# A new order of the steps in a three-batch software pipeline: a decoder of two layers on one Trainium2 core

## The reference

```python
x = ln(x + L0_attn(x))          # Nystrom attention, 16 heads of 8, 64 landmarks,
                                # 6 steps of an iterative inverse
x = ln(x + L0_xattn(x, ctx))    # cross attention, 16 heads of 8, relative bias
x = ln(x + L0_ffn(x))           # 8 experts, top 1, relu
x = ln(x + L1_attn(x))          # causal attention, 16 heads of 8
x = ln(x + L1_xattn(x, ctx))    # cross attention, 16 heads of 64, mask, its own norm
x = ln(x + L1_ffn(x))           # gelu MLP, weights composed of 32 low-rank pieces
# iterative inverse, n_iter = 6
KV = K @ V
V = (0.25 * V) @ (13 * I - KV @ (15 * I - KV @ (7 * I - KV)))
```

## Time and profile before

| | |
|---|---|
| median of 3 runs | 2584.53 us (2582.13 to 2587.29) |
| the profiled execution, its time | 2582.42 us |
| the profiled execution, its span | 2580.6 us |
| mean granted TensorE clock | 0.951 |
| PE busy | 2279.9 us |
| DVE busy | 1957.8 us |
| ACT busy | 1443.2 us |
| POOL busy | 360.0 us |

### The profile page before, as it was taken

How to read it: one execution, slowest core, us unless ns; L and a number is a source line. 1 busy time by engine, 2 the same in 40 slices (tenths; PEclk the granted TensorE clock), 3 DMA queues, 4 the chain that set the end, 5 groups by cost and what they waited for, 6 DMA issues and landing times.

```text
span 2580.6 us, 95561 instructions
## 1 busy us (share of the span) xinstructions
PE 2279.9 (88%) x40576; PEld 1845.7 (72%) x40576; DVE 1957.8 (76%) x6185; ACT 1443.2 (56%) x5093; POOL 360.0 (14%) x516
## 2 busy tenths in 40 slices
PE   6589999999999999999999999999999999999875
PEld 4467777777777777777777777777777777777763
DVE  3358887887888887788888777888877788887753
ACT  0346565655665556566555655655565565656531
POOL 0001111111111111111111111111111111111111
PEclk9589999999999999999999999999999999999995
DMA  6000000000000000000000000000000000000000
GB/s 267 5 4 7 9 9 8 9 9 5 7 9 9 9 9 9 5 7 8 8 9 8 9 5 8 8 8 9 8 9 5 8 8 9 9 8 7 4 5 3
DMA packets 29529, 35.73 MB, mean 14 GB/s; under 512 B 3240, under 2 KB 27824, under 8 KB 28464
## 3 DMA queue, kind: packets, MB, share of 16 engines
q1 hardware_dynamic: 29104, 29.62, 3.3%
HBM read 27.51 MB, written 2.10 MB: 11 GB/s over the span
## 4 chain that ended last, share of the span: by engine, by line
PE 44%; DVE 29%; ACT 18%; issue 6%; POOL 1%; DVEq 0%; ACTq 0%; POOLq 0%
PE ps L525 23%; PE ps L528 7%; ACT probs L1079 5%; PE ps L785 3%; ACT ss L993 3%; PE ps L869 3%; PE ps L802 3%; DVE probsT L1322 2%; ACT probs L1027 2%; PE ps L917 2%; ACT ey L1004 2%; DVE small L1227 2%; DVE x_rows L1186 2%; DVE small L1315 2%; DVE qk_v L1310 1%
## 5 line engine op out<-in xcount | busy, mean ns | idle before, releaser
L1027 ACT ACTIVATE probs<-ps,small 128x128 f32<-128x128 f32 x1024 | 282.5, 391 | 70.1 <-DVE small L1315 69.2
L1322 DVE COPY probsT<-ps 128x512 f32<-128x512 f32 x384 | 262.8, 684 | 75.8 <-PE ps L528 72.7
L1112 POOL TENSOR_TENSOR small<-small,weights 128x1 f32<-128x1 f32 x256 | 140.6, 549 | 1178.7 <-DVE small L1175 1178.7
L528 PE MATMUL ps<-weights,probs 128*128 128x128 f32 x1536 | 248.0, 284 | 47.1 <-POOL probs L1123 23.8
L1315 DVE TENSOR_REDUCE small<-ps 128x4 f32<-128x512 f32 x384 | 254.1, 683 | 13.0 <-PE ps L869 8.7
L528 PEld LDWEIGHTS ps<-weights,probs 128*128 128x128 f32 x1536 | 171.3, 142 | 110.4 <-POOL probs L1123 45.0
L1123 POOL TENSOR_TENSOR probs<-probs,small 128x256 f32<-128x256 f32 x128 | 108.9, 851 | 927.2 <-DVE small L1451 927.2
L1079 ACT ACTIVATE probs<-ps,small 128x128 f32<-128x128 f32 x512 | 181.3, 371 | 14.5 <-DVE small L1315 13.0
L525 PE MATMUL ps<-wz,ss 64*64 64x72 f32 x6144 | 156.0, 228 | 17.6 <-DVE wz L1269 12.2
L1268 DVE SCALAR_TENSOR_TENSOR wz<-ey,ss 128x256 f32<-128x256 f32 x320 | 147.1, 460 | 31.0 <-ACT ss L993 13.5
L989 ACT COPY ss<-ps 128x288 f32<-128x288 f32 x192 | 77.4, 403 | 158.8 <-PE ps L525 156.7
(11 more groups left out here) (200 smaller groups left out, 5288.3 us busy)
## 6 DMA issues: line engine op xcount, KB each, us to landing
weights<-in_wpack SPq DMA_DIRECT2D x1, 5703.5 KB
fc_B<-in_b SPq DMA_DIRECT2D x2, 2048.0 KB, 13.5
fc_A<-in_a SPq DMA_DIRECT2D x2, 2048.0 KB, 23.4
x_in_rows<-in_x SPq DMA_DIRECT2D x32, 64.0 KB, 1.8
x_in_T<-in_xT SPq DMA_DIRECT2D x32, 64.0 KB, 1.8
ctx_T<-in_ctxT SPq DMA_DIRECT2D x32, 64.0 KB, 1.9
ctx_rows<-in_ctx SPq DMA_DIRECT2D x32, 64.0 KB, 1.9
mask_i<-in_mask SPq DMA_DIRECT2D x32, 64.0 KB, 1.9
```

Source lines behind the costliest of these rows:

```text
L528: return nc.tensor.transpose(dst, src, ident)
L1027: ins = nc.scalar.activation(probs(s, g)[:, j], bank(s, SCORE_BANK[g], 128 * j, 128), ACT.Exp, bias=sm(s, "nb", 4 * g + j, 1), scale=-1.0)
L1112: nc.gpsimd.tensor_tensor(sm(s, out), sm(s, ve), w("mhalf"), ALU.pow).then_inc(sem(done, s), 1)
L1322: V.tensor_copy(probsT(s, n % 4).rearrange("p a b -> p (a b)"), bank(s, 2)).then_inc(sem("pT", s), 1)
```

## The change

Only the number `PERIOD` and the places in `PLACES` are new; each step has the same instructions and the same waits as before. The diff, cut to a few lines:

```diff
-PERIOD = 74.58771
+PERIOD = 74.45336
 PLACES = {
...
-        "n.proj -17.633  n.v 4.964  n.a0 6.181  n.a1 8.153  n.a2 10.438  n.a3 11.417  n.b0 14.158  n.b1 14.159  "
+        "n.proj -6.362  n.v 6.575  n.a0 6.930  n.a1 9.337  n.a2 12.675  n.a3 15.620  n.b0 17.432  n.b1 17.846  "
...
-        "r1.ctx 120.972  r1.out 150.323  rm.out 165.845  r2.xbo 194.598  r2.out 194.620  ry.stats 194.621  "
+        "r1.ctx 135.356  r1.out 154.543  rm.out 170.775  r2.xbo 198.249  r2.out 198.282  ry.stats 204.577  "
```

More of the change, by code:

```diff
@@ L64 @@
 BATCHES = B
-PERIOD = 74.58771
+PERIOD = 74.45336
 PLACES = {
     "sp": (
-        "n.xT 2.765  n.x 72.671  ",
+        "n.xT 2.607  n.x 72.513  ",
         "r1.ctxT 83.425  r1.ctx 83.485  rf.ln 233.799  ",
@@ L72 @@
     "pe": (
[16 rows of a table removed]
[16 rows of a table added]
     ),
     "act": (
[11 rows of a table removed]
[11 rows of a table added]
     ),
     "pool": (
-        "n.lm0 26.914  n.lm1 45.054  n.out 94.547  ",
-        "r1.ctx 120.972  r1.out 150.323  rm.out 165.845  r2.xbo 194.598  r2.out 194.620  ry.stats 194.621  "
-        "ry.xbo 194.622  ry.p0 215.030  ry.p1 216.541  ry.p2 234.171  ry.p3 237.043  ry.out 248.329  "
-        "rf.out 262.075  ",
+        "n.lm0 29.381  n.lm1 35.740  n.out 97.819  ",
+        "r1.ctx 135.356  r1.out 154.543  rm.out 170.775  r2.xbo 198.249  r2.out 198.282  ry.stats 204.577  "
+        "ry.xbo 209.993  ry.p0 223.550  ry.p1 225.077  ry.p2 231.021  ry.p3 241.150  ry.out 247.791  "
+        "rf.out 257.508  ",
     ),
     "dve": (
[17 rows of a table removed]
[17 rows of a table added]
     ),
```

## The result

The changed kernel took 2550.44 us (2548.0 to 2555.54, four runs), the kernel before 2585.91 in the same comparison. The ratio is 0.9867 [0.9851, 0.9882]: faster by 35 us, half of the 70 that were forecast, inside the range and at the number of rival A.

A forecast was written before the change was run, and what follows sets the result against it. No engine is full, so order and TensorE's 6.16 us idle per batch matter, plus a 1.2 us slow stretch. 29 x 2.0 = 58 us plus 10 x 1.2 = 12 us gives 70: 2514 us, range just below 2498 to 2572.

The forecast's parts named there:

- rival A: Half comes back through a mis-timed late producer: at most 1 us per batch, 34 us, 2550; chance 0.19.
- parts 1 to 3: Batch start to n.S0: moving rf.h, r1.k and n.y0 makes steps 0.54, then 0.81, then 1.09 us earlier.
- Part 1: Start of the batch, rf.h ahead of r2.e1: 0.54 us earlier.
- part 7: End of batch: r2.v fills VectorE's wait for ry.out, n.ln 2.2 us earlier; r1.ctx ahead of ry.xbo on Pool costs nothing.
- Part 4: Newton's first half: n.W00 and n.W01 no longer behind r1.e2, n.S1 at 33.1 us against 34.98, 1.9 us earlier.
- Part 6: Second half of the batch: n.S3 1.6 us earlier, n.W3 and n.S4 1.9, n.W5 2.0.
- Part 5: From r1.e3 to n.W2: new waits give back 0.6 us, leaving n.W2 1.33 us earlier.
- The slow stretch: Half-clock stretch after n.W5, costing 1.2 us: in about 13 of 29 batches instead of 23, 12 us saved.
- the 75.1 interval: Batch interval in us at which the slow stretch was said to repeat in nearly every batch; at 73.9 most escaped.
- B: PERIOD falls by 0.134 us, 4 us in all, or the interval slips back to 75.1: 2580, no change; chance 0.1.
- C: Slower: clock also falls from r1.v2 to r1.z, two slow stretches per batch, 26 us more, 2610; chance 0.09.
- D: No slow stretch at all, each batch 71.9 us: 86 us saved, 2498; chance 0.12.

The follow-up runs named there:

- the part-5 and ry.p3 experiments: Part 5 undone on the change with ry.xbo back ahead of r1.ctx: 2536.56 us; n.S51 ahead of ry.p3 on the changed kernel: 2549.05 us.
- part 1 alone: Kernel before with only rf.h moved ahead of r2.e1, n.a0 and n.v, and r2.o0 ahead of n.a1: 2563.43 us, ratio 0.9925.
- e2: No run of this name occurs in the kept text or elsewhere; only the code step r1.e2 does, so no change or time can be given.

## Where the prediction held and where it failed

**The direction and parts 1 to 3: right.** Part 1 is shown by itself at 0.54 us. At r1.s01 and n.S0 the shifts were 0.93 and 1.23 against 0.81 and 1.09. The other half of part 7 held as well: from n.W5 to the next n.proj the change gains 1.28 - 1.06 = 0.22 us, and I had given r2.v ahead of ry.out 0.2.

**Part 4: right mechanism, 0.2 too much.** n.S1 is at 33.29 and I had said 33.1. It would have been at 33.0 without Pool's swap.

**Part 7: the step that failed first.** I wrote that "Pool's swap (r1.ctx ahead of ry.xbo) costs nothing: ry.xbo is wanted 40 us later". I asked when its result is wanted and not what runs beside it. It costs 0.28 us per batch, shown by two kernels.

**Part 6: a gain that is a loss.** I put n.S4 at 1.9 us and wrote n.W5 2.0 without timing n.S50 and n.S51 behind ry.t2's copy and ry.p3 on VectorE. n.S4 was 1.35 earlier and n.W5 1.06. Undoing the part from n.S4 on makes the batch 0.20 to 0.25 us shorter, shown by two kernels.

**Part 5:** n.W2 gained 0.89 instead of 1.33. Of the missing 0.44, Pool's swap is 0.28 to 0.30. The new waits that I listed there were real, but taking out the one for r1.rows changed nothing at n.S3.

In both losses a VectorE instruction that I carried over at its old length was held up by GpSimd beside it, by 0.31 us at n.S01 and 0.35 at n.S51. At n.S01 the experiments show it as the cause; at n.S51 they don't, since taking it away alone brought 0.07. So 0.51 of the 0.72 us that the order fell short is shown. The other 0.2 stays open; the part-5 and ry.p3 experiments moved it by 0.07 at most.

**The slow stretch: the step that failed in the clock's half.** I took its number for a matter of where the fall had been before (the place around n.W5) and of the 75.1 interval, and put every other place at nothing. Around n.W5 it did become rare, 9 in 28 batches instead of 22. But 17 more fell at 1.2 to 1.6 and at 41 to 42.4 us, and the count went from 23 to 26 instead of to 13: the term of 10 x 1.2 = 12 us came out at about -5. The interval was refuted by part 1 alone. My bounds of 0 and 29 held. I also took the 5 us between three repeats for what can be told from no change; 22 executions of the same kernel lie 16 us apart.

**The rivals.** A had the time, 2550, and the right kind of reason, a late producer; its cap of 1 us per batch was close to 1.28. Its clock part had the wrong sign, so that it hit the number to the microsecond is luck: it took 29 + 5 us, where the runs show about 37 - 5. B's period of 0.134 us less was off by a factor of ten. C named the place at 42 us (r1.v2 to r1.z) and the double stretch in one batch, and both exist: 7 batches of 28 have such a pair and take 74.95 to 75.83 us, 2.3 us or more over an undisturbed one. Its condition was met by half: the order brought less than 1.4 us (1.28), but both stretches came in 7 batches and not in every one. Ahead of the stretch at 42, TensorE was busy 1.74 of 3.20 us:

```profile
2076.10:2079.30 3.20, 1.74 (x67) 1.34 (x68) 2.36 (x10) 2.88 (x13) 0.85 (x1) 1.00 0.03 5
```

D, no slow stretch, did not happen in any of the eleven changed kernels. The rule behind it, the Trainium skill's ("TensorE: Matmul & The Clock Gate", section "HAM oscillation") that idle gaps bring the fall, agrees in direction with this row and with the two busy shares near 1.9 us ahead of a fall above; the page's case is a long wait for DMA in every round, and the longest gap ahead of this row's fall is 0.85 us, ahead of the other two 1.3. It does not explain, where the engine was busy throughout.

**The checkpoints.** VectorE busy 60.5: 60.62. TensorE idle 4 us: it is 72.64 - 66.98 = 5.66, against 6.16 before. The batch fell by 1.28 but the idle time by only 0.5, since the busy time in the profile fell too, by 0.78 with the same instructions. A checkpoint on TensorE's idle time was a poor one; the starts of named steps told more. Of my four signs of being wrong three came: n.W2 gained under 1 us, two stretches lay in one batch, and n.a3 was at 8.57, not under 8.5. The last says nothing against part 1, since my own figure for it was 9.06 - 0.54 = 8.52.

## What to carry to other kernels

When an order is changed, time each moved step against what runs on the neighbouring engine at that moment, not only against when its result is wanted: a GpSimd step with forty microseconds of slack cost 0.28 us per batch by sitting beside one VectorE step on the path. Follow the shift to the last producer of the last link (here n.S51), since a gain of 1.9 us one step earlier (n.S5) says nothing about it. Where the clock falls in a few microseconds of each batch, do not forecast that a new order escapes it; price it at today's count, and test parts alone, for the best version here was the change with one part and one swap taken out.

## What the hardware showed that I had not expected

- A VectorE instruction with two inputs in SBUF (128x256) took 0.73 us instead of 0.42 beside a GpSimd add of 0.45 us and 0.83 beside a GpSimd product of 0.85, and a 128x32 one 0.54 instead of 0.19. The larger ended 0.28 us and the smaller 0.05 us after GpSimd's instruction each time. In 14 of 28 batches GpSimd's add was the one that waited, 0.74 us instead of 0.45.
- The granted clock falls to 0.50 (1.2 GHz) after stretches in which TensorE was busy 1.74 of 3.20 us as well as 3.30 of 3.30. Two more transpositions in the second kind of place all but ended the falls there (9 to 1), and others appeared elsewhere.
- A single stretch of 3.4 us at 0.50 made a batch 1.1 to 1.4 us longer where it lay at 65 to 66 us (after), and 1.4 where it lay at 41 (one batch); a pair at 1.3 and 42 made it 2.4 longer. At 1.1 us it cost 0.6 in the kernel before and 1.0 with part 1 alone. At 31 it cost 1.2 with part 1 alone, and at 31 to 33 it cost 2.2 to 3.3 in the kernel with added products, where up to 1.6 of that is a stop of TensorE (next point).
- TensorE stopped for 1.0 to 1.6 us in the middle of a run of matmuls, for nothing that the trace shows, in 5 batches of each of the two kernels with added TensorE instructions, and in one batch of the others.
